# Scores of a self attention head, issued between the two score units of a cross attention step

## The reference

```
x += cross_attention_16_heads(layernorm(x), ctx)      # 256 queries x 4096 keys, head size 16
x += self_attention_top64(layernorm(x))               # 16 heads, 256 x 256 scores; the 64 largest of a row are kept
x += routed_ffn(layernorm(x))                         # 8 experts, capacity 128
x += cross_attention_1_head(layernorm(x), ctx)        # head size 256
x += state_space_layer(layernorm(x))                  # two directions, 16 states
x += tile_ffn(x)                                      # 8 tiles, the best of each row
```

## Time and profile before

| | |
|---|---|
| Median of 3 runs | 1780.58 us |
| Profiled execution, its own time | 1785.58 us |
| Its span | 1784.0 us |
| Mean granted TensorE clock | 0.908 of full |
| TensorE, VectorE, ScalarE, GpSimd busy | 84%, 72%, 58%, 15% |

### The profile page before, as it was taken

How to read it: one execution, slowest core, us unless ns; L and a number is a source line. 1 busy time by engine, 2 the same in 40 slices (tenths; PEclk the granted TensorE clock), 3 DMA queues, 4 the chain that set the end, 5 groups by cost and what they waited for, 6 DMA issues and landing times.

```text
span 1784.0 us, 30655 instructions
## 1 busy us (share of the span) xinstructions
PE 1490.2 (84%) x11490; PEld 908.8 (51%) x11490; DVE 1293.2 (72%) x3892; ACT 1033.0 (58%) x1667; POOL 273.8 (15%) x246
## 2 busy tenths in 40 slices
PE   4999999998998988988977797778879879765766
PEld 2555566655555555555544484465456437422323
DVE  4000078897977887777988999997977884688893
ACT  2888777776766765666752353375475455425420
POOL 5000011222212122222121221210100100010000
PEclk9999999999998998899987899889989999887777
DMA  8543333123312330312104121125433423322320
GB/s 166 89 100 81 73 72 60 37 51 71 61 35 50 72 56 19 72 25 49 49 1 147 60 72 60 59 72 130 131 95 111 131 61 107 72 53 73 80 67 6
DMA packets 70869, 128.20 MB, mean 72 GB/s; under 512 B 15264, under 2 KB 38696, under 8 KB 67632
## 3 DMA queue, kind: packets, MB, share of 16 engines
q1 hardware_dynamic: 70704, 126.04, 29.8%
HBM read 124.70 MB, written 1.31 MB: 71 GB/s over the span
## 4 chain that ended last, share of the span: by engine, by line
PE 52%; DVE 19%; issue 15%; ACT 9%; POOL 2%; SPq 2%; DMA 0%; POOLq 0%; DVEq 0%; ACTq 0%
PE ps L391 18%; PE ps L403 11%; PE ps L631 4%; ACT attn_arena L1227 4%; DVE attn_late L1767 4%; DVE attn_late L1632 3%; DVE attn_top L1764 3%; PE ps L511 3%; PE ps L530 3%; PE ps L680 2%; DVE attn_late L1627 2%; PE ps L721 2%; PE ps L519 2%; PE ps L494 2%; DVE attn_mx L1576 1%
## 5 line engine op out<-in xcount | busy, mean ns | idle before, releaser
L1227 ACT ACTIVATE attn_arena<-ps 128x1024 f32<-128x1024 f32 x512 | 496.0, 1023 | 223.9 <-PE ps L391 222.0
L1764 DVE MAX8 attn_top<-attn_late 128x8 f32<-128x256 f32 x1024 | 380.9, 414 | 55.1 <-ACT attn_late L1253 55.1
L1767 DVE MATCH_REPLACE8 attn_late<-attn_top,attn_late 128x256 f32<-128x256 f32 x1024 | 411.1, 409 | 0.0
L391 PE MATMUL ps<-attn_arena 32*128 32x256 f32 x4096 | 380.9, 415 | 6.6 <-ACT attn_arena L1227 4.2
L391 PEld LDWEIGHTS ps<-attn_arena 32*128 32x128 f32 x4096 | 257.3, 191 | 82.8 <-issue 41.7
L403 PE MATMUL ps<-attn_arena 128*32 128x256 f32 x4096 | 286.3, 397 | 2.2 <-issue 1.8
L1120 POOL TENSOR_SCALAR attn_late<-attn_late 128x512 f32<-128x512 f32 x64 | 95.7, 1495 | 647.8 <-DVE attn_late L1767 647.8
L680 PE MATMUL ps<-attn_late,ident 128*128 128x512 f32 x256 | 157.4, 748 | 43.4 <-DVE attn_late L1634 43.4
L1375 ACT ACTIVATE attn_arena<-attn_early,attn_arena 128x255 f32<-128x255 f32 x256 | 109.0, 497 | 131.7 <-DVE attn_late L1632 123.8
L403 PEld LDWEIGHTS ps<-attn_arena 128*32 128x32 f32 x4096 | 110.0, 111 | 140.3 <-issue 82.1
L1632 DVE TENSOR_TENSOR_SCAN attn_late<-attn_arena,attn_late 128x1024 f32<-128x1024 f32 x64 | 147.6, 2306 | 30.8 <-PE ps L680 28.2
(11 more groups left out here) (222 smaller groups left out, 1712.0 us busy)
## 6 DMA issues: line engine op xcount, KB each, us to landing
attn_arena<-ctxT SPq DMA_DIRECT2D x128, 256.0 KB, 5.6
attn_late<-rows SPq DMA_DIRECT2D x64, 512.0 KB, 5.0
attn_arena<-ctxV SPq DMA_DIRECT2D x16, 1024.0 KB, 13.1
attn_arena<-maskT SPq DMA_DIRECT2D x32, 512.0 KB, 3.6
attn_arena<-ctx SPq DMA_DIRECT2D x32, 512.0 KB, 3.9
attn_arena<-w SPq DMA_DIRECT2D x2, 1024.0 KB
X<-x SPq DMA_DIRECT2D x4, 256.0 KB, 3.2
out<-X SPq DMA_DIRECT2D x4, 256.0 KB, 4.5
```

The lines of the kernel that those rows point to most:

```text
L391: mm = pe.matmul(ps[:, first + j - 2 * i, u * S:(u + 1) * S], kx[n % 2][rows, k0:k0 + P], qpad[rows, n % GROUPS, b * S:(b + 1) * S], start ...
L1227: act.activation(probs[m % 2][:, 2 * i:2 * i + 2], ps[:, first:first + 2, :], ACT.Exp, scale=1.0 / 16.0).then_inc(exp_done, 1)
L1764: dve.max(top[:, t, turn], s[:, i, t] if turn == 0 else work[:, i, t]).then_inc(picked, 1)
L1767: dve.match_replace(work[:, i, t], top[:, t, turn], s[:, i, t] if turn == 0 else work[:, i, t], LOW).then_inc(picked, 1)
```

## The change

`cross_scores` takes the number of a head, `between`, and issues that head's scores after its first unit. The slot 1 of p does this for head p + 1 where that head is one of the 64 and is not the first of a batch; `scores(p + 1)` at its old place, behind the products of the step before and what belongs to the one-head cross attention, is left only where no cross step is. No other instruction and no other engine's order is touched.

```diff
-            def cross_scores(m):
+            def cross_scores(m, between=None):
                 b, n, kk = m // 64, m // PAIRS_OF_KT, m % PAIRS_OF_KT
                 if kk == 0:
                     pe.wait_ge(k_loaded[n % 2], 64 * (n // 2 + 1))
                 for i in range(2):
+                    if i and between is not None:
+                        scores(between)
                     unit = 2 * m + i
                     if last_user(unit) >= 0:
                         pe.wait_ge(exp_done, last_user(unit) + 1)
...
                     m = cross_it(p, slot)
+                    early_pair = slot == 1 and 0 <= p + 1 < B * H and (p + 1) % H
                     if m is not None:
-                        cross_scores(m)
+                        cross_scores(m, p + 1 if early_pair else None)
                         if m:
                             cross_products(m - 1)
...
                     if slot == 1:
-                        if 0 <= p + 1 < B * H and (p + 1) % H:
+                        if early_pair and m is None:
                             scores(p + 1)
```

## The result

The changed kernel took 1793.0 us (median of 9 runs, 1790.07 to 1805.02); the kernel before 1780.58 (9 runs, 1773.56 to 1788.16). The ratio is 1.0078, 95% interval 1.0049 to 1.0106: some 14 us slower, inside the range, four times the forecast of +3.4 us. The profiled execution took 1793.0 us, its span is 1791.5; that of before had 1784.0. Lines have moved: scores of a head are L513 (were L511), cross scores L393 (L391), products L405 (L403), the exponential L1230 (L1227).

A forecast was written before the change was run, and what follows sets the result against it. Score units wait for ScalarE's exponentials, so TensorE time saved mostly counts for nothing; -2.7 + 0.9 + 5.2 = +3.4 us, 1784.0 against the median 1780.58 (1789.0 for an execution like the profiled), range 1769 to 1798.

The forecast's parts named there:

- What bounds the stage: Where self attention and cross steps run together: score units wait for ScalarE's exponentials, so saved TensorE time mostly counts nothing.
- (a): Moved heads not opening a group, 34: TensorE saves 0.7 us, worth nothing in 26 slots that wait for exponentials.
- rival of program order: Second score unit held behind the moved scores everywhere, matmuls starting in program order: 25.6 us slower, 1806; chance 0.08.
- (b): Six slots with a transpose or projection behind the scores (p = 13, 21, 29, 32, 36, 37): 2.7 us saved.
- (c): Two slots at half clock, p = 14 and 30: scores lengthen the second unit's chain, +0.45 us each, +0.9 together.
- (d): Nine group-opening heads: second unit and products stand behind the wait for q and k, +5.2 us (0 to 10.3).
- third rival: Wait of the group-opening heads costs its upper bound and TensorE drops to half clock more often: 1800 us; chance 0.07.
- the forecast's own range: Launch time of 1775 to 1793 us, including the case of no change at all; chance 0.72.
- signs of being wrong: Moved scores and second unit run serially on different strips, ScalarE's idle falls over 10 us, or the stage's clock changes.
- selection of head 45: Sign in the changed profile: its start should come some 3 us later than before.
- The rival that TensorE is the bound: TensorE sets the time, so all 34 heads not opening a group give 0.7 us: 1762 us; chance 0.13.

The follow-up runs named there:

- E1: Changed kernel, but only the 34 heads that do not open a group are moved, the nine openers keep their old place: 1.0005 of the kernel before.
- E10: Changed kernel with unread matmuls ahead of the wait of the nine opening heads and in the idle gaps that E9 fills: 0.998 of the kernel before, 1780.57 us.
- E9: Kernel before with unread matmuls in ten places where TensorE idled 1.5 us or more: 0.9978 of the kernel before, 1780.0 us.
- E3: Changed kernel with ScalarE writing a group's q and k before the exponentials of the head in slot 0: 0.9999 of the kernel before.
- E4: Changed kernel with five unread matmuls ahead of the wait for q and k of the nine opening heads: 1.0055 of the kernel before.
- E7: The changed kernel measured again, with no further edit: 1.0061 of the kernel before.
- E5: Kernel before with only the nine group-opening heads moved, behind the second cross score unit and ahead of the products: 1.006 of the kernel before.
- E8: Kernel before with only the nine group-opening heads moved between the units, and five unread matmuls ahead of their wait: 1.0049 of the kernel before.

## Why the prediction was right, and where its size was off

**What bounds the stage.** Right: where S was hidden under ScalarE's work and the clock was full in both profiles, p keeps its length to 0.01 us (p = 2: 15.57 in both; the same for p = 4 to 6 and 8 to 10), although TensorE has less to do. E1 shows it for the launch.

**(a)** Right: P0 1.95 us after A1, and A2 as before where the exponential ends late; in p = 5 A2 moves from 2.34 to 2.95 after A1 and p = 5 stays at 13.53. S starts ahead of instructions of A1 that stand before it in the program, and B1 is not held until S is done, so the rival of program order is out.

**(b)** The term is right where it was aimed (ScalarE's idle time in p = 36 falls by 0.63; A2 in p = 32 by 0.37, in p = 13 by 0.20). With the clock held up (E10 against E9) the six slots give 2.4 us instead of 2.7, though not shared out as forecast: p = 37 gives 0.2 instead of 0.7 and p = 29 0.9 instead of 0.2 to 0.4. In the launch it does not show: E1 keeps all of it and measures 1.0005, and its interval, which reaches to 3 us faster, would hide 2.7. In E1's profile p = 36 is 1.2 us shorter and p = 37 and 38 are 1.6 and 0.9 longer, at half clock. That they are longer because of the gain is likely, since E3, E4 and the changed kernel's first profile have the same lengths of p = 37 and 38, but E7 does not, and so it is not shown.

**(c)** Too small to be seen against the clock: p = 14 took 19.59 against 19.32, p = 30 22.67 against 20.65 with 3.4 us more at half clock.

**(d)** Right in place and mechanism, and at full clock in size: 0.50 in p = 7, 11 and 23; A2 in p = 19 and 35 0.86 later (0.85 expected); the nine slots of E10 take 5.1 more than those of E9; in p = 7 P0 starts 3.53 and A2 4.53 us after A1, where the prediction's times give 3.52 and 4.52. E5 corrects the working: I had all of it carried on by B1's exponential; holding P0 alone still costs 0.25. **The mis-sized term is the clock after the wait.** I put it at nothing, with the words that "the new gap is only 1.3 us long" and the clock 1.00 there. The earlier trace rows hold only p = 3 of the nine; the trace of before shows 1.00 in eight of them and 0.91 in p = 19, but a clock read where the gap did not yet exist says nothing of what follows the gap. The runs show that right behind this very gap the granted clock fell to half in four of the nine slots of the first profile (p = 3, 27, 39, 43), for 1.84 to 1.90 us each instead of 0.50, which is 1.34 to 1.40 more per drop; with p = 35 at 1.39 and p = 19 at 0.45 the nine cost 10.8 us, not 5.2. That is half a microsecond above the upper bound that I gave for (d), 10.3, reached by another way, and it is the third rival's kind of outcome, short of its 1800. E9 and E10 show the predicted 5.2 of the slots with the clock up.

**The sum.** +3.4 forecast; +0.6 (-2.0 to 3.2) between the launches at held clock; 11 to 14 us as launched. The range of 1769 to 1798 held the 1793.0, and this is in part luck: the forecast's own range ended at 1793, and the room above it came from rivals that I gave 0.15 together. The result reached the upper end through the clock, which is in no term of the sum. Of the signs of being wrong, one came: the clock of the stage fell from 0.96 to 0.94 in the first profile (in E7 it is 0.96). The selection of head 45 begins 5.9 us later than before in the first profile, not 3, and 3.1 us earlier in E7, so this sign tells nothing at the size of the forecast. The two measures of the changed kernel, 1.0078 and 1.0061, agree within their intervals. The rival that TensorE is the bound is out (E1).

What stays open is the split of the remaining few us of the launch: the opening slots account for 9 to 11, less the gains of (b); E4 and E8 took half of that away in the slots and only a part of it in the launch, and the drops at the batch ends differ from profile to profile.

## What to carry to other kernels

Before an instruction is moved ahead of others on an in-order queue, list what it waits for and what would then stand behind that wait; here nine of 43 moves crossed a wait for another engine, and those nine alone made the loss. The producer of the awaited data can often be moved as well: two lines on ScalarE took the whole loss back. And price a new gap on TensorE with both clocks: here the wait cost 0.50 us at full clock and 1.84 to 1.90 at half.

## What the runs showed of the hardware

- Matmuls on different strips of 32 rows do not start in program order: with three chains issued as A1 (8 instructions), S (4), B1 (8), S starts 0.02 us after A1 and ahead of instructions of A1 that start 0.32 us after it, each strip then going 0.21 to 0.22 us from start to start.
- A wait of TensorE holds what is behind it on other strips too: in p = 7 of the changed kernel S, on strip 0, waits until 335.52, and B1, on strips 2 and 3, starts at 335.54; in E5, where B1 stands ahead of the wait, it runs on behind A1 without a gap.
- A gap of 1.32 us, after 1.13 us of two-strip work, was followed by a granted clock of 0.50 in 11 of 27 slots of three profiled executions (p = 3 of the changed kernel) and of 1.00 in the others (p = 7 of the same execution), with the same work around them. The clock fell while TensorE was at work again, 0.06 to 1.52 us after the gap's end. With unread matmuls in the same gap it fell behind none of the 27 of E4, E8 and E10.
- Unread matmuls in the idle gaps of one stage made the kernel before 0.2% faster (0.9978, 0.9957 to 0.9999), and the time of that stage 12 us shorter in the one profile.
